# Loads of x and stores of the result in two parts of two token tiles, stores in the order of their making, last sums in two parts

## The chip, the cores and the metric

One core of a Trainium2 chip. The time is that of one execution on the device, in microseconds; the median of the runs is the kernel's time. All inputs lie in HBM when the clock starts and the result has to lie there when it stops.

## What is computed

Four layers of gated cross-attention and feed-forward over two sequences of 512 tokens, each token a row of 128 numbers in fp32. Each stage norms x, computes a branch and adds it with a gain:

```python
x = x + jnp.tanh(g_xattn[0]) * _L0_xattn_ref(_layernorm(x, axis=-1), ctx_1024, ctx_1024, mask_Bx1xSxS2_if1, ...)
x = x + jnp.tanh(g_ffn[0]) * _L0_ffn_ref(_layernorm(x, axis=-1), L0_ffn_w1, L0_ffn_b1, L0_ffn_w2, L0_ffn_b2)
...
x = x + jnp.tanh(g_xattn[3]) * _L3_xattn_ref(_layernorm(x, axis=-1), ctx_1024, L3_xattn_Wq, ...)
x = x + jnp.tanh(g_ffn[3]) * _L3_ffn_ref(_layernorm(x, axis=-1), L3_ffn_rhs)
return x
```

The layers are dense attention with a mask and an MLP (0), multi-query attention and a top-2 mixture of experts with a shared one (1), attention and a top-1 mixture (2), and three rounds of slot attention with a GRU and then a product of int8-quantised rows (3). This last one ends the program:

```python
q_lhs = jnp.clip(jnp.round(lhs / lhs_scale), -INT8_MAX, INT8_MAX).astype(jnp.int8)
q_rhs = jnp.clip(jnp.round(rhs / rhs_scale), -INT8_MAX, INT8_MAX).astype(jnp.int8)
acc = jax.lax.dot_general(q_lhs, q_rhs, (((2,), (0,)), ((), ())), preferred_element_type=jnp.int32)
return acc.astype(jnp.float32) * lhs_scale * rhs_scale
```

## The kernel before

The two sequences ("halves" in the code, index b) are 512 tokens each, held on chip as x[128 partitions, b, 4 token tiles, 128]. Partition p of tile t holds token 128 t + p. A token row is one piece of 512 bytes in HBM, so a load or store of one sequence is 256 KB in 512 such rows.

The work is cut into steps (all_steps, from line 150): a name, a sequence, an engine, an assumed duration and the steps it follows. A planner (schedule, line 308) puts every engine's steps into one fixed order, ORDERS, from the assumed durations, a table of due times for steps that need a load (LOADED, line 88) and a table of delays, LATER. The two sequences interleave on all engines. Where PE would idle, the planner puts in filler matmuls (keep_warm) that have no reader. Inside one engine the order is the program's; between engines there are only semaphores. The eight PSUM banks are dealt out by the same planner: `banks.full(name)` is a wait for PE to have filled a bank, `banks.emptied(name)` one for its reader to have drained it.

SP issues all DMAs, from one queue, in the order that is written in its block (line 726 on). Loads come first: x of sequence 0, small constants, the query weights, the context, the mask (line 738), the constant halves (740), more weights, x of sequence 1, the bias rows (747), then the weights of the later layers. After one more load in the middle of the program (line 761) SP waits for each sequence's `x_final`, sequence 0 first, stores it, and waits for both stores.

At the start DVE takes statistics of x (norm, lines 1401 and 1404, two token tiles at a time), POOL turns a variance into a reciprocal root (lines 789 and 790), behind fourteen memsets of its own (817 to 830), DVE norms the tiles (1410), converts the mask (1462, 1463), prepares the keys (1447 to 1455) and then takes sixteen maxima of scores (1537). ACT copies PSUM banks out (1232, 1236) and makes gains from the bias rows (1254).

At the end, for each sequence, DVE makes integers (integers, 1420 to 1424), PE transposes them (937) and ACT copies them out; DVE clamps them (turn, 1728), PE multiplies them (846), and quantised (1730) does the rest on DVE: four scalings of one token tile each out of PSUM (1735), and one sum of all four tiles into x (1739). The planner's order has sequence 1 before sequence 0 there. The sum waits for the drain of the bank that the last scaling signals:

```python
                last.then_inc(drained["dve"], 1)
                dve.wait_ge(*banks.emptied("out", 7, b))
                V.scalar_tensor_tensor(flat(x[:, b, :, :]), flat(xn[:, b, :, :]), gain[:, g:g + 1],
                                       flat(x[:, b, :, :]), ALU.mult, ALU.add).then_inc(x_final[b], 1)
```

Of the kernel before, what the change touches and what calls it, by code (L numbers as in the profile page):

```python
# [7 lines left out]
ALU = mybir.AluOpType  # L8
# [7 lines left out]
P = 128  # L16
B = 2
# [38 lines left out]
PACKS = {  # L56
    "attn0": [("wq", GROUPS * GR), ("wv", D), ("wo", D)],
    "ffn0": [("w1", W0), ("w2", C0 * D)],
    "attn1": [("wk", GROUPS * GR), ("wv", D), ("wq", GROUPS * GR), ("wo", D)],
    "ffn1": [("gates", E1 + 1), ("w_g", C1 * P), ("w_u", C1 * P), ("w_down", C1 * D), ("s_g", SH), ("s_u", SH),  # L60
             ("s_down", len(SHC) * D)],
    "attn2": [("wk", GROUPS * GR), ("wv", D), ("wq", GROUPS * GR), ("wo", D)],
    "ffn2": [("router", E2), ("w1", C2 * P), ("w2", C2 * D), ("bias2", D)],
    "attn3": [("wk", D), ("wv", D), ("wq", D), ("wi", 3 * D), ("wh", 3 * D), ("rhs_t", D)],
# [421 lines left out]
ORDERS, DEALT, IDLE_FILLERS = schedule()  # L486
# [41 lines left out]
def program(nc, a, out):  # L528

    with ExitStack() as ctx:  # L530
# [7 lines left out]
        x = sb("x", [P, B, T, D])  # L538
# [5 lines left out]
        cols = sb("cols", [P, cols_n])  # L544
        rows = sb("rows", [P, rows_n])
        consts = sb("consts", [P, const_n])
        ctx_t = sb("ctx_t", [P, B * CTX])
        ctx_rows = sb("ctx_rows", [CTX, B, D])
# [25 lines left out]
        ctx_4 = sb("ctx_4", [P, B, GKP])  # L574
# [81 lines left out]
        def by_tile(tile):  # L656
# [10 lines left out]


        loaded = {k: sem("loaded_" + k) for k in
                  ["x_0", "x_1", "ident", "wq0", "ctx_4", "bv", "cols", "rows", "consts", "rounded", "halves", "ctx_t", "ctx_rows", "mask"] + list(PACKS)}  # L670
        filled = sem("bank_filled")
        drained = {"act": sem("bank_drained_by_act"), "dve": sem("bank_drained_by_dve")}
        consts_made = sem("consts_made")
# [17 lines left out]
        def per_half(name):  # L691
            return [sem(f"{name}_{b}") for b in range(B)]
# [20 lines left out]
        lhs_ready = per_half("lhs_ready")  # L713
        n_ready = per_half("n_ready")
        slots_ready = per_half("slots_ready")
        x_final = per_half("x_final")
        stored = sem("stored")

# [7 lines left out]
        @block.sync  # L726
        def _(sp):
            def load_x(b):
                sp.dma_start(x[:, b, :, :], a["x"][b].rearrange("(t p) d -> p t d", p=P)).then_inc(loaded[f"x_{b}"], 16)

            wq_n = columns(PACKS["attn0"])[0]["wq"][1]
            load_x(0)
            sp.dma_start(cols[:, :], a["cols"]).then_inc(loaded["cols"], 16)
            sp.dma_start(consts[:, 0:P], a["consts"][:, 0:P]).then_inc(loaded["ident"], 16)
            sp.dma_start(packs["attn0"][:, 0:wq_n], a["attn0"][:, 0:wq_n]).then_inc(loaded["wq0"], 16)
            sp.dma_start(ctx_t[:, :], a["ctx_t"]).then_inc(loaded["ctx_t"], 16)
            sp.dma_start(consts[:, P:const_n], a["consts"][:, P:const_n]).then_inc(loaded["consts"], 16)
            sp.dma_start(mask_i[:, :, :, :], a["mask"].rearrange("b o (t p) k -> p b (o t) k", p=P))\
              .then_inc(loaded["mask"], 16)
            sp.dma_start(halves[:, :], a["halves"].bitcast(BF16)).then_inc(loaded["halves"], 16)  # L740
            sp.dma_start(packs["attn0"][:, wq_n:], a["attn0"][:, wq_n:]).then_inc(loaded["attn0"], 16)
            for i in range(B):
                sp.dma_start(ctx_4[:, i, 0:GK].rearrange("p (h k) -> p h k", h=LH),
                             a["ctx_t"][:, i * CTX:(i + 1) * CTX].unsqueeze(1).broadcast_to([P, LH, CTX]))\
                  .then_inc(loaded["ctx_4"], 16)
            load_x(1)
            sp.dma_start(rows[:, :], a["rows"].broadcast_to([P, rows_n])).then_inc(loaded["rows"], 16)
            bv_at = rows_at["bv0"][0]
            sp.dma_start(bv_cols[:, :], a["rows"][:, bv_at:bv_at + 3 * D].rearrange("o (l d) -> d (o l)", l=3),
                         allow_slow_non_contiguous=True)\  # L750
              .then_inc(loaded["bv"], 16)
            sp.dma_start(packs["attn1"][:, :], a["attn1"]).then_inc(loaded["attn1"], 16)
            sp.dma_start(packs["attn2"][:, :], a["attn2"]).then_inc(loaded["attn2"], 16)
            sp.dma_start(packs["ffn0"][:, :], a["ffn0"]).then_inc(loaded["ffn0"], 16)
            sp.dma_start(rounded_in[:, :], a["rounded"].bitcast(BF16)).then_inc(loaded["rounded"], 16)
            sp.dma_start(ctx_rows[:, :, :], a["ctx_rows"].rearrange("b k d -> k b d")).then_inc(loaded["ctx_rows"], 16)
            sp.dma_start(packs["attn3"][:, :], a["attn3"]).then_inc(loaded["attn3"], 16)
            sp.dma_start(packs["ffn1"][:, :], a["ffn1"]).then_inc(loaded["ffn1"], 16)
            for b in range(B):
                sp.wait_ge(*banks.full("out", 1, b))  # L760
            sp.dma_start(packs["ffn2"][:, :], a["ffn2"]).then_inc(loaded["ffn2"], 16)
            for b in range(B):
                sp.wait_ge(x_final[b], 1)
                sp.dma_start(out[b].rearrange("(t p) d -> p t d", p=P), x[:, b, :, :]).then_inc(stored, 16)
            sp.wait_ge(stored, 16 * B)

        def spread_keys(engine, layer, k_part, keys, ready):

# [617 lines left out]
        def _(dve):  # L1386
            V = nc.vector
# [8 lines left out]
            def norm(b, stage, h):  # L1396
                tiles = range(2 * h, 2 * h + 2)
                if stage == 0:
                    dve.wait_ge(loaded[f"x_{b}"], 16)
                for t in tiles:  # L1400
                    last = V.bn_stats(stats[:, b, t, :], x[:, b, t, :])  # L1401
                link(last)
                for t in tiles:
                    last = V.bn_aggr(mv[:, b, t, :], stats[:, b, t, :])  # L1404
                last.then_inc(var_ready[b], 1)
# [25 lines left out]
            def flat(tile):  # L1431
                return tile.rearrange("p t d -> p (t d)")
# [297 lines left out]
            def quantised(b):  # L1730
                g = GAIN_OF[7]
                dve.wait_ge(*banks.emptied("rscale"))
                dve.wait_ge(*banks.full("out", 7, b))
                for t in range(T):
                    last = V.scalar_tensor_tensor(xn[:, b, t, :], banks.bank("out", 7, b)[:, t * P:(t + 1) * P],  # L1735
                                                  route_s[:, b, 3, t:t + 1], rscale_b[:, :], ALU.mult, ALU.mult)
                last.then_inc(drained["dve"], 1)
                dve.wait_ge(*banks.emptied("out", 7, b))
                V.scalar_tensor_tensor(flat(x[:, b, :, :]), flat(xn[:, b, :, :]), gain[:, g:g + 1],  # L1739
                                       flat(x[:, b, :, :]), ALU.mult, ALU.add).then_inc(x_final[b], 1)  # L1740

            mine = {"norm": norm, "norm_end": norm_end, "integers": integers, "keys_in": keys_in, "mask_parts": mask_parts, "values_in": values_in,
                    "out_bias": out_bias, "slots_in": slots_in, "query": query, "maxima": maxima, "sum_rows": sum_rows, "spread": spread,
# [111 lines left out]
```

## Time and profile before

| | us |
|---|---|
| median of 3 runs | 345.37 |
| the three runs | 344.36, 345.45, 345.37 |
| the profiled execution | 344.06 |
| its span, first to last instruction | 342.1 |
| mean granted clock of PE, of full speed | 0.983 |

The profile is of one more execution than the three runs; its time is 344.06, of which the span is 342.1. Durations in the rows come from that execution. PE is TensorE's matmuls, DVE VectorE, ACT ScalarE, POOL GpSimd, SPq the queue of SyncE, which issues the DMAs. PE is busy 92% of the span, fillers included, DVE 65%, ACT 40%, POOL 17%. DMA works in the first 30 us, a little at 74 to 80 and at the very end.

### The profile page before, as it was taken

To read this page: it belongs to the slowest core of one execution; us is meant where nothing else is said; L and a number is where in the kernel's file an instruction comes from. 1 tells how busy PE (TensorE), PEld (TensorE's weight loads), DVE (VectorE), ACT (ScalarE), POOL (GpSimd) and SP (SyncE) were. 2 spreads that over 40 slices of the span, in tenths; PEclk is the share of its full clock that TensorE was granted. 3 is DMA by queue.
4 is the path that set the end of the run, shared out by engine and by line. 5 is a ranking of instruction groups with operands and counts; after the bars stand their busy time and mean duration, and the time that the engine had idled before them with its cause. 6 is when DMAs were issued, how large, how long until landed. Compare 5 with 4: busy or idle time off the path is not lost. (4 is left out here: it accounts for less than half of the span.)

```text
span 342.1 us, 5510 instructions
## 1 busy us (share of the span) xinstructions
PE 314.4 (92%) x2028; PEld 191.0 (56%) x2045; DVE 223.5 (65%) x634; ACT 135.5 (40%) x283; POOL 57.8 (17%) x107
## 2 busy tenths in 40 slices
PE   8889799997799999999999779999999989998983
PEld 3543544773434554656887443447769776766441
DVE  4971952769804598763588970446361889999994
ACT  1245173223366646422002255632232466757200
POOL 7131050352001021000030300012021211111220
PEclk9999999999899999999999978999999999999999
DMA  7970000021000000000000000000000000000002
GB/s 186 318 284 0 2 2 0 1 82 54 2 0 2 0 2 0 1 2 0 0 2 0 1 2 0 3 2 0 2 0 2 0 1 2 0 0 2 0 1 61
DMA packets 6958, 8.70 MB, mean 25 GB/s; under 512 B 3067, under 2 KB 5781, under 8 KB 6677
## 3 DMA queue, kind: packets, MB, share of 16 engines
q1 hardware_dynamic: 6933, 8.37, 7.3%
q8 instruction: 16, 0.26, 0.3%
q14 instruction: 9, 0.07, 0.1%
HBM read 7.84 MB, written 0.52 MB: 24 GB/s over the span
## 5 line engine op out<-in xcount | busy, mean ns | idle before, releaser
L1232 ACT ACTIVATE wide<-psum 128x512 f32<-128x512 f32 x72 | 37.2, 603 | 22.3 <-PE psum L846 22.3
L846 PE MATMUL psum<-xn_t,w_ffn 128*128 128x512 f32 (+1 forms) x88 | 41.2, 596 | 0.0
L1537 DVE TENSOR_REDUCE mx<-psum 128x4 f32<-128x308 f32 x96 | 38.2, 469 | 1.8 <-PE psum L846 1.4
L789 POOL TENSOR_SCALAR nw<-mv 128x2 f32<-128x2 f32 x32 | 7.0, 218 | 189.9 <-DVE mv L1404 189.9
L1232 ACT ACTIVATE q<-psum 128x512 f32<-128x512 f32 (+1 forms) x36 | 20.9, 595 | 27.3 <-PE psum L846 21.6
L846 PE MATMUL psum<-wide 78*128 78x386 f32 (+1 forms) x69 | 25.4, 505 | 3.2 <-DVE wide L1688 1.9
L846 PEld LDWEIGHTS psum<-early,wide 128*128 128x128 f32 x192 | 24.8, 191 | 4.9 <-issue 3.8
L846 PE MATMUL psum<-halves 128*128 128x512 bf16 x110 | 27.2, 379 | 0.4 <-issue 0.2
L1543 DVE RECIPROCAL rinv<-psum 128x64 f32<-128x64 f32 x6 | 3.3, 556 | 36.6 <-PE psum L1023 36.6
L846 PE MATMUL psum<-xn_t,early 128*128 128x512 f32 x52 | 26.5, 601 | 0.1
L846 PE MATMUL psum<-early,wide 128*128 128x128 f32 x192 | 25.3, 275 | 0.2
L846 PEld LDWEIGHTS psum<-w_ffn,wide 128*128 128x128 f32 (+1 forms) x176 | 22.4, 192 | 4.4 <-issue 3.0
L1410 DVE TENSOR_SCALAR xn<-x,mv,nw 128x128 f32<-128x128 f32 x64 | 19.0, 341 | 8.8 <-POOL nw L790 8.7
L846 PE MATMUL psum<-w_ffn,wide 128*128 128x128 f32 (+1 forms) x176 | 23.1, 276 | 0.7 <-DVE wide L1618 0.5
L790 POOL TENSOR_TENSOR nw<-nw,minus_half 128x2 f32<-128x2 f32 x32 | 23.0, 720 | 2.7
L846 PEld LDWEIGHTS psum<-xn_t,w_ffn 128*128 128x128 f32 (+1 forms) x88 | 15.3, 188 | 13.4 <-issue 10.8
L846 PEld LDWEIGHTS psum<-w_attn,q 128*128 128x128 f32 x176 | 20.8, 192 | 2.7 <-ACT wide L1232 1.7
L846 PE MATMUL psum<-w_attn,q 128*128 128x128 f32 x176 | 22.2, 277 | 0.1
L1232 ACT ACTIVATE xn_t<-psum 128x512 f32<-128x512 f32 x18 | 10.5, 596 | 26.9 <-PE psum L937 18.4
L846 PE MATMUL psum<-wide,heads_of 128*32 128x512 f32 x144 | 20.0, 630 | 0.0
L1612 DVE TENSOR_TENSOR wide<-q,psum 128x512 f32<-128x512 f32 (+1 forms) x22 | 14.7, 682 | 7.9 <-ACT q L1232 4.9
L846 PE MATMUL psum<-wide,v_cols 128*32 128x512 f32 x144 | 19.0, 600 | 0.3 <-ACT wide L1232 0.3
(222 smaller groups left out, 517.2 us busy)
## 6 DMA issues: line engine op xcount, KB each, us to landing
w_ffn<-in_ffn SPq DMA_DIRECT2D x1, 2088.5 KB, 13.6
early<-in_ffn SPq DMA_DIRECT2D x1, 1104.0 KB, 5.0
w_attn<-in_attn SPq DMA_DIRECT2D x1, 640.0 KB, 8.2
w_attn<-in_attn SPq DMA_DIRECT2D x2, 288.0 KB, 6.9
x<-in_x SPq DMA_DIRECT2D x2, 256.0 KB, 3.8
early<-in_ffn SPq DMA_DIRECT2D x1, 512.0 KB, 8.0
out<-x SPq DMA_DIRECT2D x2, 256.0 KB, 2.6
rows<-in_rows SPq DMA_DIRECT2D x1, 468.0 KB, 6.3
```

Of the source, the lines that this page charges most:

```text
L789: link(G.tensor_scalar(nw[:, b, 0, tiles], mv[:, b, tiles, 1], LN_EPS, None, ALU.add))
L790: G.tensor_tensor(nw[:, b, 2, tiles], nw[:, b, 0, tiles], minus_half[:, tiles], ALU.pow)\
L846: return nc.tensor.matmul(out_, lhs, rhs, start=start, stop=stop, **kw)
L1232: A.activation(dst, banks.bank(*name)[0:rows_, 0:cols_], fn, **kw).then_inc(drained["act"], 1)
L1410: last = V.tensor_scalar(xn[:, b, t, :], x[:, b, t, :], mv[:, b, t, 0:1], nw[:, b, 2, t:t + 1], ALU.subtract, ALU.mult)
L1537: last = V.tensor_reduce(mx[:, b, t, lane_heads(g)], banks.bank("max", layer, b, t, g)[:, 0:GK].rearrange("p (h k) -> p h k", k=CTX), AX.X ...
L1543: V.reciprocal(rinv[:, b, :, :], banks.bank("sum_t", layer, b).rearrange("p (t h d) -> p t h d", t=T, h=H)[:, :, :, 0])\
L1612: V.tensor_tensor(wide[0:r, b, at_, :], act_s[k % 2][0:r, b, :], banks.bank("up", b, k)[0:r, :], ALU.mult)\
```

## The change

A load of x for one sequence becomes two loads of two token tiles, each with a semaphore; the statistics of two tiles wait for their own load. The stores become two per sequence, each of two tiles, in the order in which DVE's own list has the sequences. In quantised the second scaling signals `scaled_back`; the last sum is split into two of two tiles, the first waiting for that signal, the second for the drain as before, and each signals x_final.

```diff
             def load_x(b):
-                sp.dma_start(x[:, b, :, :], a["x"][b].rearrange("(t p) d -> p t d", p=P)).then_inc(loaded[f"x_{b}"], 16)
+                for h in range(2):
+                    tiles = slice(2 * h, 2 * h + 2)
+                    sp.dma_start(x[:, b, tiles, :], a["x"][b].rearrange("(t p) d -> p t d", p=P)[:, tiles, :])\
+                      .then_inc(loaded[f"x_{b}_{h}"], 16)
...
-            for b in range(B):
-                sp.wait_ge(x_final[b], 1)
-                sp.dma_start(out[b].rearrange("(t p) d -> p t d", p=P), x[:, b, :, :]).then_inc(stored, 16)
-            sp.wait_ge(stored, 16 * B)
+            for b in (b for phase, b, _ in ORDERS["dve"] if phase == "quantised"):
+                for h in range(2):
+                    tiles = slice(2 * h, 2 * h + 2)
+                    sp.wait_ge(x_final[b], h + 1)
+                    sp.dma_start(out[b].rearrange("(t p) d -> p t d", p=P)[:, tiles, :], x[:, b, tiles, :]).then_inc(stored, 16)
+            sp.wait_ge(stored, 2 * 16 * B)
...
                 if stage == 0:
-                    dve.wait_ge(loaded[f"x_{b}"], 16)
+                    dve.wait_ge(loaded[f"x_{b}_{h}"], 16)
...
                     last = V.scalar_tensor_tensor(xn[:, b, t, :], banks.bank("out", 7, b)[:, t * P:(t + 1) * P],
                                                   route_s[:, b, 3, t:t + 1], rscale_b[:, :], ALU.mult, ALU.mult)
+                    if t == 1:
+                        last.then_inc(scaled_back[b], 1)
                 last.then_inc(drained["dve"], 1)
-                dve.wait_ge(*banks.emptied("out", 7, b))
-                V.scalar_tensor_tensor(flat(x[:, b, :, :]), flat(xn[:, b, :, :]), gain[:, g:g + 1],
-                                       flat(x[:, b, :, :]), ALU.mult, ALU.add).then_inc(x_final[b], 1)
+                for h in range(2):
+                    tiles = slice(2 * h, 2 * h + 2)
+                    if h:
+                        dve.wait_ge(*banks.emptied("out", 7, b))
+                    else:
+                        dve.wait_ge(scaled_back[b], 1)
+                    V.scalar_tensor_tensor(flat(x[:, b, tiles, :]), flat(xn[:, b, tiles, :]), gain[:, g:g + 1],
+                                           flat(x[:, b, tiles, :]), ALU.mult, ALU.add).then_inc(x_final[b], 1)
```

The instructions of PE, ACT and POOL are the same, in the same order. Line numbers behind the edit are six or more higher in the changed kernel (1735 is 1741, 1739 is 1752, 764 is 770).

SP's queue at the start of the program, before:

```order
L729 DMA x<-in_x 128x4x128
L733 DMA cols<-in_cols 128x32
L734 DMA consts<-in_consts 128x128
L735 DMA early<-in_attn 128x160
L736 DMA ctx_t<-in_ctx_t 128x154
L737 DMA consts<-in_consts 128x112
L738 DMA early<-in_mask 128x8x77
```

and in the changed kernel:

```order
L732 DMA x<-in_x 128x2x128 x2
L737 DMA cols<-in_cols 128x32
L738 DMA consts<-in_consts 128x128
L739 DMA early<-in_attn 128x160
L740 DMA ctx_t<-in_ctx_t 128x154
L741 DMA consts<-in_consts 128x112
L742 DMA early<-in_mask 128x8x77
```

Everything behind the load of x, the mask among it, stands one issue later; the same happens once more at x of sequence 1.

SP's queue at the end, before:

```order
L758 DMA w_ffn<-in_ffn 128x4177
L761 DMA early<-in_ffn 128x2208 [waits bank_filled]
L764 DMA out<-x 128x4x128 [waits x_final_0]
L764 DMA out<-x 128x4x128 [waits x_final_1]
L530 UNCONDITIONAL_BRANCH [waits stored]
```

and in the changed kernel:

```order
L762 DMA w_ffn<-in_ffn 128x4177
L765 DMA early<-in_ffn 128x2208 [waits bank_filled]
L770 DMA out<-x 128x2x128 [waits x_final_1] x2
L770 DMA out<-x 128x2x128 [waits x_final_0] x2
L530 UNCONDITIONAL_BRANCH [waits stored]
```

The stores are four, and sequence 1's come before SP's wait for sequence 0.

DVE at the end of the program, before; the first scalings and sum are sequence 1's, nothot_t is the clamp of sequence 0:

```order
L1735 SCALAR_TENSOR_TENSOR xn<-psum,route_s,rscale_b 128x128 [waits bank_filled,bank_drained_by_act]
L1735 SCALAR_TENSOR_TENSOR xn<-psum,route_s,rscale_b 128x128 x3
L1739 SCALAR_TENSOR_TENSOR x<-xn,gain,x 128x512 [waits bank_drained_by_dve]
L1728 TENSOR_SCALAR nothot_t<-nothot_t 128x512 [waits bank_drained_by_act]
L1735 SCALAR_TENSOR_TENSOR xn<-psum,route_s,rscale_b 128x128 [waits bank_filled,bank_drained_by_act]
L1735 SCALAR_TENSOR_TENSOR xn<-psum,route_s,rscale_b 128x128 x3
L1739 SCALAR_TENSOR_TENSOR x<-xn,gain,x 128x512 [waits bank_drained_by_dve]
```

and in the changed kernel:

```order
L1741 SCALAR_TENSOR_TENSOR xn<-psum,route_s,rscale_b 128x128 [waits bank_filled,bank_drained_by_act]
L1741 SCALAR_TENSOR_TENSOR xn<-psum,route_s,rscale_b 128x128 x3
L1752 SCALAR_TENSOR_TENSOR x<-xn,gain,x 128x256 [waits scaled_back_1]
L1752 SCALAR_TENSOR_TENSOR x<-xn,gain,x 128x256 [waits bank_drained_by_dve]
L1734 TENSOR_SCALAR nothot_t<-nothot_t 128x512 [waits bank_drained_by_act]
L1741 SCALAR_TENSOR_TENSOR xn<-psum,route_s,rscale_b 128x128 [waits bank_filled,bank_drained_by_act]
L1741 SCALAR_TENSOR_TENSOR xn<-psum,route_s,rscale_b 128x128 x3
L1752 SCALAR_TENSOR_TENSOR x<-xn,gain,x 128x256 [waits scaled_back_0]
L1752 SCALAR_TENSOR_TENSOR x<-xn,gain,x 128x256 [waits bank_drained_by_dve]
```

The first half's sum still stands behind all four scalings; only its wait is for an earlier one.

## Rows read from the trace of the kernel before

**Rows 1.** Chain that ended last, 335 to 342: start us, us, what
```profile
335.68 0.21 DVE nothot_t L1728
...
336.03 0.40 PE psum L846 x4
...
336.52 1.14 DVE xn L1735 x4
...
337.68 0.75 DVE x L1739
```

**Rows 2.** Waits of SP: who waited for whom, us in total, times, longest
```profile
SPq L764 <- DVE x L1739: 264.3, 1, 264.3
...
SPq L530 <- DMA out<-x: 2.3, 1, 2.3
```

**Rows 3.** Timeline, 333 to 342: start us, us, instruction, [idle before <-releaser]
```profile
333.77 1.12 DVE L1735 SCALAR_TENSOR_TENSOR xn<-psum,route_s,rscale_b 128x128 f32<-128x128 f32 x4
...
338.46 0.95 SPq L764 DMA_DIRECT2D out<-x  x2
```

**Rows 4.** Windows 339.0 to 341.7: busy us, PEclk, DMA share, GB/s
```profile
339.00:339.40 0.40, 0.00 (x0) 0.00 (x0) 0.00 (x0) 0.00 (x0) 0.00 (x0) 1.00 0.00 1
339.40:341.30 1.90, 0.00 (x0) 0.00 (x0) 0.00 (x0) 0.00 (x0) 0.00 (x0) 0.91 0.93 275
341.30:341.70 0.40, 0.00 (x0) 0.00 (x0) 0.00 (x0) 0.00 (x0) 0.00 (x0) 0.50 0.01 3
```

**Rows 5.** Timeline, 0 to 14, columns as in rows 3
```profile
3.64 0.43 SPq L738 DMA_DIRECT2D early<-in_mask  x1
...
3.92 0.95 POOL L830 MEMSET nothot_t<- 128x1024 bf16 x1
...
4.06 0.25 DVE L1404 BATCH_NORM_AGGREGATE mv<-stats 128x2 f32<-128x6 f32 x2
...
4.92 0.22 POOL L789 TENSOR_SCALAR nw<-mv 128x2 f32<-128x2 f32 x1
...
5.97 0.60 DVE L1410 TENSOR_SCALAR xn<-x,mv,nw 128x128 f32<-128x128 f32 x2 [1.01 <-POOL nw L790]
...
7.49 0.31 DVE L1462 TENSOR_SCALAR mask_b<-early 128x308 bf16<-128x308 int32 x1
...
8.41 0.17 DVE L1447 TENSOR_REDUCE lane_mask<-consts 128x4 f32<-128x16 f32 x1
...
8.87 0.24 DVE L1450 CAST k_hi<-k_t 128x154 fp32r<-128x154 f32 x1 [0.29 <-ACT k_t L1236]
```

**Rows 6.** Line 764, the stores: duration ns min/median/max, and landing
```profile
L764 SPq DMA_DIRECT2D out<-x x2: 398/452/507, 338.5 to 338.9; - x2
...
DMA to landing us min/median/max: 2.4/2.6/2.8
```

**Rows 7.** Lines 1735 and 1739: duration ns min/median/max, first and last start
```profile
L1735 DVE SCALAR_TENSOR_TENSOR xn<-psum,route_s,rscale_b x8: 340/343/350, 333.8 to 337.3; 128x128 f32<-128x128 f32 x8
...
L1739 DVE SCALAR_TENSOR_TENSOR x<-xn,gain,x x2: 752/752/752, 334.9 to 337.7; 128x512 f32<-128x512 f32 x2
```

**Rows 8.** DMA issues, from the page: KB, us from issue to landing
```profile
early<-in_mask SPq DMA_DIRECT2D x1, 308.0 KB, 3.7
...
cols<-in_cols SPq DMA_DIRECT2D x1, 16.0 KB, 2.5
```

**Rows 9.** Windows: length, busy us of PE, PEld, DVE, ACT, POOL, PEclk, DMA, GB/s
```profile
12.00:20.00 8.00, 6.17 (x50) 4.19 (x47) 7.96 (x26) 0.93 (x3) 0.00 (x0) 1.00 1.02 383
...
88.00:91.75 3.75, 1.89 (x28) 1.02 (x24) 3.12 (x9) 2.06 (x4) 0.00 (x0) 1.00 0.00 0
...
201.00:207.70 6.70, 5.88 (x36) 2.88 (x40) 2.89 (x8) 3.23 (x7) 0.00 (x0) 0.50 0.00 0
```

**Rows 10.** Timeline, 12 to 22, columns as in rows 3
```profile
13.12 0.21 ACT L1254 ACTIVATE gain<-rows 128x8 f32<-128x8 f32 x1 [1.00 <-DMA rows<-in_rows]
...
20.17 1.02 PE L846 MATMUL psum<-mask_t,halves 77*128 77x512 bf16 x4 [0.38 <-ACT mx_t L1232]
```

More of the change, by code:

```diff
@@ L669, in program @@
         loaded = {k: sem("loaded_" + k) for k in
-                  ["x_0", "x_1", "ident", "wq0", "ctx_4", "bv", "cols", "rows", "consts", "rounded", "halves", "ctx_t", "ctx_rows", "mask"] + list(PACKS)}
+                  ["x_0_0", "x_0_1", "x_1_0", "x_1_1", "ident", "wq0", "ctx_4", "bv", "cols", "rows", "consts", "rounded", "halves", "ctx_t", "ctx_rows", "mask"] + list(PACKS)}
         filled = sem("bank_filled")
@@ L715, in program @@
         slots_ready = per_half("slots_ready")
+        scaled_back = per_half("scaled_back")
         x_final = per_half("x_final")
```

## Prediction

> **What bounds the kernel now.** The change touches both ends of the program and nothing between, so I read the two ends. The chain that ended last [rows 1] shows the tail: PE multiplies sequence 0's quantised rows at 336.03, DVE scales the four token tiles from 336.52, and one 512-wide sum on DVE runs 337.68 to 338.43. SP's waits [rows 2] and the timeline [rows 3] show what hangs on that. SP waited 264.3 us for L1739 and then issued both stores together at 338.46. Sequence 1 was finished first (its four scalings start at 333.77, its sum is done at 335.68), but SP stands on sequence 0's semaphore, so a finished 256 KB waits 2.8 us for nothing. After 338.46 + 0.95 = 339.41 SP waits 2.3 us, to 341.71, for the landings. The span ends 0.4 later.
>
> The windows of the last microseconds [rows 4] cut that end into three: 0.94 us from the first issue to the first bytes (nothing moves before 339.40), 1.90 us at a 0.93 share of the 16 DMA engines and 275 GB/s, which is the whole 0.524 MB, and 0.41 us from the last bytes (341.30) to SP's release. So 1.90 of the 3.3 us behind DVE is bandwidth over both sequences' bytes.
>
> At the front I read the timeline [rows 5]. DVE has its first x statistics done at 4.06 + 0.25 = 4.31, but POOL is in its last memset until 3.92 + 0.95 = 4.87 and takes the statistics at 4.92. POOL releases DVE at 5.97, not the load of x.
>
> **The change, part by part.**
>
> Stores in finishing order. Sequence 1's parts leave at about 335.3 and 335.8, and are through before 338, beside DVE and PE work. What remains behind the end of DVE is 256 KB in place of 512: half of 1.90, a gain of 0.95 us. Each issue takes 0.40 to 0.51 us [rows 6] and SP has nothing else to do then; the two more issues cost nothing there.
>
> Last sums in two parts. A 128x128 scaling takes 343 ns, the 128x512 sum 752 [rows 7]; the slope is 409/384 = 1.07 ns a column, so a 256-wide sum takes about 480. Four scalings take 1.13 [rows 1, 3]: independent ones start (1.13 - 0.343)/3 = 0.26 apart, that is 0.08 before the last ends, while the sum, which waits for the last scaling, starts 0.03 after it. The first half now waits for the second scaling only, so it starts at 337.65 - 0.08 = 337.57 and ends at 338.05; the second starts 0.40 later and ends at 338.45. Against 338.43 the split costs 0.02: the fixed cost of one more instruction (752 - 2 x 480, that is 0.21) is paid by the two overlaps, 0.11 and 0.08. The same holds at sequence 1, where DVE's own clamp of sequence 0 (L1728, on the chain at 335.68 [rows 1]) is next. Bounds: -0.05 each, and +0.2 each if neither overlap comes. I take 0 to 0.05 for both together.
>
> Store in two parts. The first part is issued at 338.05 + 0.03 = 338.08, in place of 338.46: 0.38 earlier. The second follows an issue later, at 338.53 (the two issues before stood 0.44 apart), with its sum done at 338.45. First bytes at 338.08 + 0.94 = 339.02, then 256 KB without a gap, 0.95, to 339.97; release at 340.38. Against 341.71: 1.33 us, of which 0.95 are bytes and 0.38 the earlier first part. With the splits' cost I take **1.3** for the tail. Bounds: 1.35 above; below, the landing of the second part. The trace has no 128 KB store; its 256 KB stores landed 2.4 and 2.8 us after issue [rows 6], the second because it queued behind the first. With 2.8 from 338.53 the gain is 0.4, with 2.4 it is 0.8. I take 1.85: 0.94 + 0.48 + 0.41 = 1.83, and the undisturbed 2.4 less half its bytes' time, 0.48, gives 1.9.
>
> The Trainium skill, "DMA: Bandwidth & Descriptors", section "Anatomy of one DMA — SWDGE (gpsimd) path", gives a fixed cost of about 2.0 us and then bytes over 436 GB/s, and lays most of the 2 us on the write's receipt; an estimate by it puts a 128 KB store at 2.3 us and the tail's gain at 0.9 instead of 1.3. The trace differs in the split: 0.41 us passed between the last bytes and the release [rows 4].
>
> Loads of x in two parts. The first half would be there about 0.5 us sooner (half of 256 KB), but POOL takes it at 4.92 either way: gain 0. The extra issue pushes every later load by about 0.48 us, those behind x_1 by 0.95. One of them has no slack. The mask is issued at 3.64 and lands 3.7 later, at 7.34 [rows 8], and DVE converts it at 7.49 without a pause [rows 5]. It now lands at about 7.82, DVE starts at 7.86, 0.37 late. Behind the four conversions stand the 8.41 reduction and then 0.29 us of idle before 8.87, where ACT's k_t is awaited: that absorbs 0.27 of it, and the cast starts **0.1** late. Who waits for that: DVE is busy 7.96 of 8.00 us in 12 to 20 [rows 9], so its sixteen maxima end 0.1 later, then ACT's mx_t, then PE at 20.17 [rows 10]. I carry all of it to the end. Bounds: 0, and 0.7 (the mask slipping by both extra issues' time, 0.95, less the 0.27). The others are covered: the bias rows land 0.95 later, and ACT, which waits for them at 13.12 [rows 10], has nothing behind that but mx_t, made after the maxima; x_1's statistics stand behind the sixteen maxima too.
>
> Sum: 1.3 - 0.1 = **1.2 us**. The profiled execution took 344.06 (span 342.1 and 2.0 around it); it would take 342.9. It lies 1.3 below the median, 345.37, near the lowest run, 344.36. From the median: **344.2 us**, 0.35% less. The bound between faster and the same is 0.3%, 1.04 us here, about what a measurement of this kernel can tell from no change.
>
> **The rivals.**
>
> *A store has a price that halving does not cut.* If a 128 KB store lands in 2.4 us, like the 256 KB one (and a 16 KB load took 2.5 [rows 8]), the second part is there at 340.93: tail 0.8, net 0.7, 344.7, the same. Against it: the 1.90 us of saturated engines, which must shrink with the bytes. For it: small loads are no quicker, though they queued behind others. The Trainium skill's page named above, "DMA: Bandwidth & Descriptors", stands on this side.
>
> *The late mask costs more.* Loads share the engines, and the mask's row comes from a queue with no second x part in it. At the bound of 0.7 the net is 0.6: 344.8, the same. For it: DVE's backlog from 8.87 on has no other slack. Against: the bytes ahead of the mask are the same.
>
> *Slower: PE's clock falls once more.* The granted clock is 1.00 in 12 to 20, where PE was busy 6.17 of 8 us waiting for DVE's maxima. It fell after 88 to 91.75, where PE was busy 1.89 of 3.75, and once more at 201, where it stayed at 0.50 for 6.7 us [rows 9], which is the 1.2 GHz level. If DVE's delay stretches PE's waits at 12 to 20, or moves a later stretch over the edge, work at half speed costs half the low stretch: 3.35 us for one like 201's. Net +2.15: 347.5, slower. It decides from a low stretch of 4.5 us (2.24 lost: the gain and 1.04). Against: PE is far busier there than before the falls, and the delay is 0.1 us. The other sign is as possible: a low stretch shortened gives 1 to 2 us more than forecast, near 342.9.
>
> *The early half of x counts.* Only if POOL were not what releases DVE; the memset's end excludes it but for hundredths. Up to 0.5 more: 343.7, faster.
>
> That the stores don't change order is excluded: SP's own order shows sequence 1 first.
>
> **How the numbers follow.** Forecast 0.52 (343.9 to 344.3, 344.2 the likeliest). Flat store price 0.20, late mask 0.13, both same. Slower clock 0.06; shorter low stretch 0.05; early x 0.04. Faster 0.52 + 0.05 + 0.04 = 0.61, less 0.03 for a forecast that lands just inside the bound: 0.58. Same 0.20 + 0.13 + 0.03 = 0.36. Slower 0.06. The range: above to a tail of 0.4 with the mask at 0.4, 345.4; below, 343.1, to the best tail (1.35, nothing at the front) and a median near the low runs, since the four executions shown spread over 1.4 us. Outside lie the clock cases and a little more.
>
> **What would show it.** Right: SP's wait for x_final ends near 335.3; four issues, two of them near 338.1 and 338.5; DMA busy about 0.95 us at the end, SP released some 1.9 us after its last issue; DVE's two 256-wide sums ending within 0.05 of where the one did; POOL still taking x's statistics at 4.92; a DVE idle of about 0.3 before the mask conversion, and the cast 0.1 late. Wrong: a last store that lands 2.4 us or more after its issue, PE or DVE further behind than 0.1 by 20 us, or a low-clock stretch that the kernel before did not have.

## The result and the profile after

| | before | changed |
|---|---|---|
| median, us | 344.33 (22 runs) | 342.85 (22 runs) |
| lowest and highest | 342.68, 345.45 | 341.51, 345.40 |
| profiled execution, us | 344.06 | 342.90 |
| its span | 342.1 | 341.0 |

The ratio is 0.9956, with a 95% interval of 0.9939 to 0.9973: less time, by 0.44% or 1.5 us, and clear of no change. It is not clear of the 0.3% that the prediction takes as its bound for faster: the interval begins at 0.27%. The three runs of before that stood ahead of the prediction had a median of 345.37; nineteen more brought it to 344.33.

The tail of the changed kernel, from its timeline (columns as in rows 3), the waits of SP, the four stores by line, and the windows of the last transfer (columns as in rows 4), in this order:

```profile
334.46 0.69 ACT L1238 ACTIVATE nothot_t<-psum,round_col 128x512 bf16<-128x512 f32 x1 [2.74 <-PE psum L943]
335.00 0.87 DVE L1752 SCALAR_TENSOR_TENSOR x<-xn,gain,x 128x256 f32<-128x256 f32 x2
335.50 3.64 SPq L770 DMA_DIRECT2D out<-x  x4
335.79 0.28 DVE L1734 TENSOR_SCALAR nothot_t<-nothot_t 128x512 bf16<-128x512 bf16 x1
...
336.71 1.13 DVE L1741 SCALAR_TENSOR_TENSOR xn<-psum,route_s,rscale_b 128x128 f32<-128x128 f32 x4 [0.64 <-PE psum L852]
337.75 0.87 DVE L1752 SCALAR_TENSOR_TENSOR x<-xn,gain,x 128x256 f32<-128x256 f32 x2
```

```profile
SPq L770 <- DVE x L1752: 264.0, 2, 261.8
...
SPq L530 <- DMA out<-x: 1.4, 1, 1.4
```

```profile
L770 SPq DMA_DIRECT2D out<-x x4: 372/434/471, 335.5 to 338.7; - x4
...
DMA to landing us min/median/max: 1.9/1.9/1.9
```

```profile
336.40:337.60 1.20, 0.20 (x4) 0.03 (x1) 0.89 (x4) 0.00 (x0) 0.00 (x0) 1.00 0.77 219
339.10:340.20 1.10, 0.00 (x0) 0.00 (x0) 0.00 (x0) 0.00 (x0) 0.00 (x0) 1.00 0.84 238
340.20:340.60 0.40, 0.00 (x0) 0.00 (x0) 0.00 (x0) 0.00 (x0) 0.00 (x0) 1.00 0.01 1
```

Against [rows 1 to 4]: sequence 1's stores leave from 335.50 and move between 336.4 and 337.6, beside DVE's and PE's work. DVE's last sum ends at 337.75 + 0.87 = 338.62; 0.5 us later bytes move, 1.1 us long in place of 1.9, and the span ends at 340.98. Before, DVE ended at 338.43 and the span at 342.10. From DVE's last end to the span's end there were 3.67 us; now 2.36. That is 1.31 us. The split of the last sums is free: first scaling to last sum took 1.91 us before (336.52 to 338.43) and takes 1.91 now (336.71 to 338.62).

The span is only 1.1 shorter, because DVE's end moved back by 0.19. That isn't from the front, since by 20 us PE stands where it stood. It appears behind the low stretch of PE's clock at 201: from 20 us up to there PE's matmuls stand in both profiles within 0.04 us of each other, but for the 0.3 us inside the low stretch at 92. The front, from the timeline:

```profile
2.82 0.49 DVE L1407 BATCH_NORM_STATS2 stats<-x 128x6 f32<-128x128 f32 x2 [1.71 <-DMA x<-in_x]
...
4.93 0.22 POOL L795 TENSOR_SCALAR nw<-mv 128x2 f32<-128x2 f32 x1
...
7.51 0.31 DVE L1468 TENSOR_SCALAR mask_b<-early 128x308 bf16<-128x308 int32 x1
...
9.04 0.24 DVE L1456 CAST k_hi<-k_t 128x154 fp32r<-128x154 f32 x1 [0.45 <-ACT k_t L1242]
```

The statistics start at 2.82 in place of 3.54, and POOL takes them at 4.93, as before [rows 5]. The mask was issued at 4.13, landed in 3.3 us and not in 3.7, and did not delay DVE at all in this execution. The cast is 0.17 late because ACT's k_t is, and k_t because PE's key matmul is. That in turn is PE's clock, whose level the matmuls' own durations show (the trace has no clock record before the first rise, and prints 1.00 there): the warm-up matmuls, line 852, 4 to 8 us:

```profile
L852 PE MATMUL psum<-wide x12: 379/634/634, 3.7 to 7.9; 128*128 128x512 bf16 x12
```

They take 634 ns at the low level, 1.2 GHz, and 379 at 2.4 GHz. The change from one to the other came at 6.4 us in the profile before and at 6.8 here, and PE's instructions are the same up to there. By 20.18 PE starts its first scores as it did at 20.17 [rows 10]. The 0.17 is not absorbed by a wait: from the cast to the first scores pass 11.00 to 11.14 us in this profile and the twelve of the experiments, and 11.30 in that of before, which happened to lose there what the changed kernel had lost already.

### The profile page after: what moved, and what is told of

The parts are those of the page before. It is cut to its first block and busy times, and to the rows that moved or that the text cites. A ratio compares the mean times of both kernels' runs of the same rounds, so it can differ in the third digit from the quotient of the medians.

```text
span 341.0 us, 5516 instructions
## 1 busy us (share of the span) xinstructions
PE 314.7 (92%) x2028; PEld 190.9 (56%) x2045; DVE 223.8 (66%) x636; ACT 135.6 (40%) x283; POOL 57.9 (17%) x107
## 3 DMA queue, kind: packets, MB, share of 16 engines
HBM read 7.84 MB, written 0.52 MB: 25 GB/s over the span
## 5 line engine op out<-in xcount | busy, mean ns | idle before, releaser
L852 PE MATMUL psum<-wide,heads_of 128*32 128x512 f32 x144 | 20.4, 640 | 0.0
```

The lines of the kernel that those rows point to most:

```text
L852: return nc.tensor.matmul(out_, lhs, rhs, start=start, stop=stop, **kw)
```

## The experiments

All of them are told by the same few readings. "Mask" is the start of the mask's conversion on DVE, "scores" that of PE's first score matmul (mask_t,halves), "DVE end" the end of the last sum, "tail" the span's end less DVE's end, "low clock" the time at half clock before DVE's end, from windows of granted clock. The ratio is against the kernel before on the same chip, whose median was 344.45 for e1 to e4, 344.20 for e5 to e7, 343.79 for e8 to e11 and 344.17 for e12; medians of different groups are therefore not to be subtracted. The columns from mask to tail are from one profiled execution each.

| kernel | median | ratio, 95% | mask | scores | low clock | DVE end | tail |
|---|---|---|---|---|---|---|---|
| before | 344.33 | | 7.49 | 20.17 | 10.2 | 338.43 | 3.67 |
| changed | 342.85 | 0.9956, 0.9939 to 0.9973 | 7.51 | 20.18 | 10.2 | 338.62 | 2.36 |
| e1 order of stores | 343.18 | 0.9965, 0.9946 to 0.9985 | 7.48 | 19.61 | 17.1 | 339.47 | 2.72 |
| e2 change, x whole | 343.07 | 0.9952, 0.9930 to 0.9973 | 7.64 | 20.28 | 10.2 | 338.79 | 2.37 |
| e3 x in parts only | 343.90 | 0.9986, 0.9972 to 1.0000 | 7.94 | 20.07 | 6.8 | 337.73 | 3.66 |
| e4 parts, old order | 344.40 | 0.9998, 0.9977 to 1.0020 | 8.25 | 20.39 | 17.1 | 340.37 | 3.47 |
| e5 POOL freed | 343.17 | 0.9972, 0.9952 to 0.9992 | 7.90 | 20.03 | 10.2 | 339.56 | 2.48 |
| e6 change again | 343.36 | 0.9970, 0.9950 to 0.9991 | 8.74 | 20.87 | 10.2 | 339.33 | 2.36 |
| e7 change, spare | 339.67 | 0.9862, 0.9839 to 0.9886 | 8.08 | 20.39 | 0 | 335.70 | 2.36 |
| e8 before, spare | 340.79 | 0.9907, 0.9886 to 0.9928 | 7.49 | 20.19 | 0 | 335.46 | 3.65 |
| e9 order, spare | 339.99 | 0.9885, 0.9863 to 0.9907 | 7.49 | 19.61 | 0 | 334.91 | 2.73 |
| e10 x in parts, spare | 340.94 | 0.9917, 0.9893 to 0.9941 | 7.49 | 19.98 | 0 | 335.27 | 3.66 |
| e11 change, spare | 339.42 | 0.9875, 0.9851 to 0.9898 | 7.84 | 19.98 | 0 | 335.29 | 2.36 |
| e12 best | 339.12 | 0.9852, 0.9819 to 0.9885 | 7.49 | 19.62 | 0 | 334.86 | 2.37 |

**e1, the order of the stores alone.**

```diff
-            for b in range(B):
+            for b in (b for phase, b, _ in ORDERS["dve"] if phase == "quantised"):
                 sp.wait_ge(x_final[b], 1)
```

> Only the order of the two whole stores is changed (sequence 1's before sequence 0's); loads, sums and store sizes are those of the kernel before. Theory (the time behind DVE's last sum is bytes plus fixed parts): sequence 1's 256 KB leave at about 335.7 and are gone by 338; behind DVE's end remain 0.03 + 0.94 + 0.95 + 0.41 = 2.3 us in place of 3.28, so 0.95 to 1.0 us less, 0.28% of the time. Rival (a store has a price that does not shrink with what is queued): the last store lands 2.8 us after its issue as before, and the gain is only the one issue, 0.44 us. Rival (the gain came from the earlier loads or from something in the middle): no gain here, ratio 1.000.

The tail fell from 3.67 to 2.72, by 0.95: the theory's number, and the price rival's 0.44 is out. Each whole store now lands by itself in 2.3 us; before it was 2.4 and 2.8 [rows 6]:

```profile
L764 SPq DMA_DIRECT2D out<-x x2: 394/396/399, 336.7 to 339.5; - x2
...
DMA to landing us min/median/max: 2.3/2.3/2.3
```

Its DVE end, though, was 1.0 later than before's, with no edit there. What differs is the table's low clock column.

**e2, the change with x loaded whole** (the load part taken back, the rest kept).

```diff
-                for h in range(2):
-                    tiles = slice(2 * h, 2 * h + 2)
-                    sp.dma_start(x[:, b, tiles, :], a["x"][b].rearrange("(t p) d -> p t d", p=P)[:, tiles, :])\
-                      .then_inc(loaded[f"x_{b}_{h}"], 16)
+                sp.dma_start(x[:, b, :, :], a["x"][b].rearrange("(t p) d -> p t d", p=P)).then_inc(loaded[f"x_{b}"], 16)
...
-                    dve.wait_ge(loaded[f"x_{b}_{h}"], 16)
+                    dve.wait_ge(loaded[f"x_{b}"], 16)
```

> The change without its load part: x is loaded whole per sequence; the stores and last sums are those of the change. Theory (the split loads are worth nothing, since POOL takes the first statistics at 4.92 either way, and whatever they cost is absorbed before 25 us): as fast as the change, 1.3 us less than before behind DVE's end (1.98 us from DVE's last end to the release in place of 3.28), ratio to before 0.996. Rival (the split loads bring the 0.2 us by which the median fell more than the 1.3 of the tail): 0.2 to 0.4 us slower than the change. Rival of the forecast (the later mask costs 0.1): 0.1 us faster than the change, with the key cast at 8.87 and not 9.04.

Tail 2.37, ratio 0.9952: the stores and sums carry the whole gain, as far as twelve runs with an interval of 0.2% to each side can tell. The cast stood at 9.15 with whole loads, behind a k_t that was done at 9.04, so the change's 9.04 was not the loads' doing.

**e3, the loads alone** (the first hunk of the change and its wait, nothing else).

> The load part alone: x in two parts, all at the end as before. Theory: no difference, ratio 1.000 within 0.1%; the first statistics on DVE start near 2.8 instead of 3.54, POOL still takes them at 4.92, and by 25 us every engine stands where it stood. The tail is 3.28 us from DVE's last end to SP's release. If the early microseconds differ from before, it is by the moment at which PE's clock rises (the warm-up matmuls go from 427 to 216 ns apart at 6.44 before, at 6.79 in the change), and the key cast moves with that moment and not with the mask's landing, which should be near 7.4. Rival (the late mask): the cast is 0.1 or more late whenever the clock rises. Rival (the earlier x counts): 0.2 to 0.5 us faster.

Tail 3.66, as before. The ratio's interval ends at 1.0000, which settles neither a small gain nor none; e10 asks again. Here DVE did wait for the mask:

```profile
7.94 0.32 DVE L1465 TENSOR_SCALAR mask_b<-early 128x308 bf16<-128x308 int32 x1 [0.37 <-DMA early<-in_mask]
```

**e4, parts in the old order** (e2 with `for b in range(B)` around the stores).

> Last sums and stores in two parts as in the change, but SP waits for sequence 0 first, as before; x is loaded whole. All 512 KB then leave behind DVE's first half sum of sequence 0. Theory: the first bytes move 0.38 us sooner than before, and the rest is 1.90 us of transfer as before, if four issues at 0.44 us keep ahead of it (the fourth is issued 1.32 us after the first, its bytes due 1.43 after the first's): 2.9 us from DVE's last end to the release, 0.35 us less than before, ratio 0.999. Rival (each further store costs its own time on the engines): as slow as before or 0.1 to 0.3 us slower.

Tail 3.47, 0.20 less and not 0.35. SP's four issues in the timeline and the stores' windows (columns as in rows 4) show why:

```profile
339.50 0.87 DVE L1749 SCALAR_TENSOR_TENSOR x<-xn,gain,x 128x256 f32<-128x256 f32 x2
340.00 1.99 SPq L767 DMA_DIRECT2D out<-x  x4
```

```profile
341.40:341.80 0.40, 0.00 (x0) 0.00 (x0) 0.00 (x0) 0.00 (x0) 0.00 (x0) 1.00 0.87 255
341.80:342.20 0.40, 0.00 (x0) 0.00 (x0) 0.00 (x0) 0.00 (x0) 0.00 (x0) 1.00 0.86 241
342.20:342.60 0.40, 0.00 (x0) 0.00 (x0) 0.00 (x0) 0.00 (x0) 0.00 (x0) 1.00 0.83 224
```

Four issues take 1.99 us, 0.50 each where I had 0.44, and 128 KB take 0.48 to move at the rate of [rows 4]: the engines were busy 0.83 to 0.87 where the two whole stores kept them at 0.93. The queue's issue rate and the bytes are about even at 128 KB, so parts in the old order give little. That smaller parts would give less is an estimate from these numbers; none were run.

**e5, POOL freed at the front.**

```diff
-            G.memset(comb_t[:, :, :].bitcast(F32), 0.0)
-            G.memset(nothot_t[:, :, :], 0.0).then_inc(zeros_made, 1)
...
-            for phase, b, args in ORDERS["pool"]:
+            for i, (phase, b, args) in enumerate(ORDERS["pool"]):
+                if i == 2:
+                    G.memset(comb_t[:, :, :].bitcast(F32), 0.0)
+                    G.memset(nothot_t[:, :, :], 0.0).then_inc(zeros_made, 1)
                 mine[phase](b, *args)
```

> The change, with POOL's last two memsets (comb_t and nothot_t, 0.95 us each) moved behind the first norm of sequence 0, so that POOL can take the first statistics at about 3.6 and not 4.92. Theory (the front is held by POOL first, and by the mask's landing, ACT's table load and PE's key matmul right behind it): DVE norms x's first tiles near 4.7 instead of 5.97, so the early half of x now shows; but ACT's k_t, the mask conversion and the key cast stand where they stood (k_t at 8.4 to 8.6, the cast near 9), and the maxima start at 12.1 to 12.3 as before. Time as the change, within 0.2%. Rival (the x chain is what the front waits for): the maxima start 0.5 us or more sooner and the time falls by 0.5 us, 0.15%.

```profile
3.88 0.22 POOL L795 TENSOR_SCALAR nw<-mv 128x2 f32<-128x2 f32 x1 [0.78 <-DVE mv L1411]
...
4.93 0.60 DVE L1417 TENSOR_SCALAR xn<-x,mv,nw 128x128 f32<-128x128 f32 x2 [0.53 <-POOL nw L796]
...
5.85 0.95 POOL L839 MEMSET comb_t<- 128x1024 f32 x1
...
5.93 1.91 DVE L1417 TENSOR_SCALAR xn<-x,mv,nw 128x128 f32<-128x128 f32 x2 [0.40 <-POOL nw L796]
...
6.74 0.95 POOL L840 MEMSET nothot_t<- 128x1024 bf16 x1
...
7.54 0.39 ACT L1243 ACTIVATE k_t<-psum,cols 128x154 f32<-128x154 f32 x1
...
7.90 0.32 DVE L1469 TENSOR_SCALAR mask_b<-early 128x308 bf16<-128x308 int32 x1
...
9.03 0.24 DVE L1457 CAST k_hi<-k_t 128x154 fp32r<-128x154 f32 x1
```

DVE norms x a whole microsecond earlier, at 4.93 in place of 5.98, and the cast stands where it stood. The early x shows once POOL is out of its way, and is then lost at the mask, which landed at 7.87. It isn't lost at k_t, as I had expected: k_t was done at 7.54 + 0.39 = 7.93, a microsecond before the cast, because PE's clock rose at 3.9 here. Nor is the test clean. The norms of the other two tiles took 1.84 and 1.65 us where they take 0.34 in every other profile, and ended at 7.84, beside the two memsets that were moved to 5.85 to 7.69. Even an earlier mask would have found DVE busy until then. That the memsets hold the norms up is read from this one profile and not tested. Scores at 20.03, ratio 0.9972, no faster than the change.

**e6, the change again.**

> The changed kernel once more, with nothing altered, for two questions: what its gain is on this chip beside the kernel before, and what moves the time from one execution to the next. Theory: from DVE's last end to the span's end 2.36 us again, as in the other executions with these stores, whatever the time is; ratio to before 0.995 to 0.997. The place of DVE's last end varies between executions by 1 to 2 us with PE's low-clock stretches (10.2 us of them in the change's first profile, 17.1 in two others), whose place follows the moment at which the clock first rose. Rival (the spread is noise of the start and end of an execution): DVE's last end is at 338.6 again within 0.2 whatever the clock does.

The tail is 2.36 again, the theory's number. DVE's end is 0.71 later than in the first profile with the same 10.2 us of low clock, so the theory's account of the spread was incomplete: this time it was the mask.

```profile
8.74 0.32 DVE L1468 TENSOR_SCALAR mask_b<-early 128x308 bf16<-128x308 int32 x1 [1.16 <-DMA early<-in_mask]
...
9.87 0.24 DVE L1456 CAST k_hi<-k_t 128x154 fp32r<-128x154 f32 x1
```

```profile
20.87 0.81 PE L852 MATMUL psum<-mask_t,halves 77*128 77x512 bf16 x3 [0.21 <-ACT mx_t L1238]
```

It landed at 8.7, and the scores started at 20.87, 0.69 late, which the end shows whole.

**e7, spare matmuls in PE's waits.** The change and 17 fillers:

```diff
+            SPARE = {(0, 1, 2): 1, (1, 1, 2): 1, (1, 1, 3): 5, (0, 2, 0): 3, (0, 2, 2): 2, (0, 2, 3): 5}
+
             def maxima(b, layer, t):

-                bks = [start_unit("max", layer, b, t, g) for g in range(LANES)]
+                bks = [start_unit("max", layer, b, t, 0)]
+                for _ in range(SPARE.get((b, layer, t), 0)):
+                    mm(bks[0], halves[:, 0:P], halves[:, 0:S])
+                bks += [start_unit("max", layer, b, t, g) for g in range(1, LANES)]
```

> The change, with 17 more filler matmuls of 512 columns (results unused) inside PE's waits at the maxima of layers 1 and 2: into the first bank of a group as soon as it is free, while PE waits for the other three. PE idles there 0.5 to 1.3 us at a time, and both low-clock stretches before the end began there. Theory (the low clock follows those idle waits, and costs what separates executions: 337.7 us at DVE's last end with 6.8 us of low clock, 338.4 to 338.8 with 10.2, 339.5 and 340.4 with 17.1): one or both low stretches go or shrink, DVE ends near 336.5 to 337.5, and the time falls 1 to 2 us below the change. Rival (PE isn't on the path in the low stretches, or the fillers delay the score matmuls behind them): no difference or 0.3 to 1 us slower, the low stretches unchanged.

More than the 1 to 2 us below the change that I expected: 339.67 against 343.36 for e6 on the same chip, and against 344.20 for the kernel before. The five runs lie within 0.65 us where before's 23 spread over 2.9; e11, the same kernel again, will show a wider spread. The windows of the changed kernel, then those of e7 (columns as in rows 9):

```profile
88.00:92.00 4.00, 2.14 (x29) 1.27 (x29) 3.39 (x9) 2.06 (x4) 0.00 (x0) 1.00 0.00 0
...
92.10:95.50 3.40, 3.40 (x28) 1.47 (x20) 1.15 (x3) 2.15 (x5) 0.00 (x0) 0.50 0.02 5
201.30:208.20 6.90, 6.35 (x40) 3.25 (x44) 2.64 (x7) 2.96 (x6) 0.00 (x0) 0.51 0.00 0
```

```profile
88.00:92.00 4.00, 3.69 (x34) 1.74 (x35) 3.39 (x9) 2.06 (x4) 0.00 (x0) 1.00 0.02 4
199.00:203.00 4.00, 3.65 (x31) 1.66 (x31) 3.36 (x9) 2.00 (x5) 0.00 (x0) 1.00 0.00 0
```

PE is busy 3.69 of 4 us where it was busy 2.14, and the clock stays at its upper level, 2.4 GHz, to DVE's end in this execution.

**e8 to e11, the parts of the change on this steadier ground.** e8 is the kernel before with the 17 fillers, e9 is e1 with them, e10 is e3 with them, e11 is e7 again.

> The kernel before with the 17 spare filler matmuls, and nothing of the change: the base on which the parts of the change can be told apart, because without low-clock stretches five runs of the change with them lay within 0.65 us. Theory: no low clock, 339.67 + 1.3 of tail - 0.2 to 0.3 of loads = 340.7 to 341.0, spread under 1 us, 3.67 us from DVE's last end to the span's end. Rival (the spare matmuls work only together with the change): low stretches again and 343 or more.

> The spare matmuls and the order of the two whole stores alone. Theory: 0.95 us less than the kernel before with spare matmuls (0.28%): 339.8 to 340.0. Rival: 0.44 us less.

> The spare matmuls and the split loads of x alone. The mask's conversion on DVE began at 7.48, 7.49, 7.64 and 8.25 in the profiles with whole loads, at 7.51, 7.90, 7.94, 8.08 and 8.74 with split ones: 0.3 later on the mean, and the change's second profile carried 0.7 us of it to PE's first scores (20.87 against 20.17). Theory now: the split loads cost 0.2 to 0.4 us against the kernel before with spare matmuls, since nothing hides the mask. Rival (what I took from the first profile, all absorbed before 25 us): no difference within 0.1 us. Rival (the 0.9986 of the loads alone was a gain): 0.3 to 0.5 us faster.

> The change with the spare matmuls again, beside its parts on one chip. Theory: 1.3 us of tail less what the loads cost, 1.0 to 1.2 us faster than the kernel before with spare matmuls, 339.5 to 339.9; the two measured parts and the halves of stores and sums (0.35) add up to it. Rival (0.44% from the 22 runs is the change's own gain): 1.5 us or more.

By medians on one chip: order -0.80, loads +0.15, the whole change -1.37. By profiles: tail -0.92, +0.01 and -1.29. And between scores and DVE's end the four profiles and e7's have 315.27, 315.30, 315.29, 315.31 and 315.31 us, whatever part of the change is in: the middle of the program is untouched to 0.04 us. The medians still carry the start of the scores, which moves between 19.6 and 20.4; six runs don't average that out, so that the loads' +0.15 is a possible cost, not a shown one (e3 alone had 0.9986, the other way). The whole change came out 0.2 above my expectation's upper end for the gain, within the same scatter.

Where the spare matmuls gain is seen by laying DVE's instructions of e8 beside the same ones of before. From 37 to 93 us they stand within 0.03 us of each other, from 102 to 195 e8's are 0.91 to 0.94 earlier, and from 214 to the end 2.96 to 3.00. The gain arises at the two low stretches and nowhere else, 0.9 us for the first (3.4 us long) and 2.0 for the second (6.8 us). The kernel before says the same without any spare matmuls: of its 78 runs beside e1 to e12, the 17 with a mean granted clock of 0.986 to 0.989 have a median of 343.16 us, the 7 at 0.974 one of 345.47.

The spare matmuls don't hold the clock up in every execution. Of the 34 runs of e7 to e12, 31 had a mean granted clock of 0.995 or more; one of e9, one of e10 and one of e11 had 0.990, 0.989 and 0.991 and took 340.78, 341.88 and 341.00 us, 0.8 to 1.6 above their kernels' medians. With that one e11 spread over 1.8 us, where the same kernel had spread over 0.65 in e7.

**e12, the version that the runs point to.** e7 with x loaded whole, and the mask ahead of cols, ident and consts in SP's queue:

```diff
             load_x(0)
-            sp.dma_start(cols[:, :], a["cols"]).then_inc(loaded["cols"], 16)
-            sp.dma_start(consts[:, 0:P], a["consts"][:, 0:P]).then_inc(loaded["ident"], 16)
...
-            sp.dma_start(consts[:, P:const_n], a["consts"][:, P:const_n]).then_inc(loaded["consts"], 16)
...
             sp.dma_start(mask_i[:, :, :, :], a["mask"].rearrange("b o (t p) k -> p b (o t) k", p=P)).then_inc(loaded["mask"], 16)
+            sp.dma_start(cols[:, :], a["cols"]).then_inc(loaded["cols"], 16)
+            sp.dma_start(consts[:, 0:P], a["consts"][:, 0:P]).then_inc(loaded["ident"], 16)
+            sp.dma_start(consts[:, P:const_n], a["consts"][:, P:const_n]).then_inc(loaded["consts"], 16)
```

> What the runs point to: the spare matmuls, the stores in order and in two parts with the last sums in two parts, x loaded whole, and SP's queue at the start reordered so that the mask stands fourth (behind x, the query weights and the context) and not seventh. Theory: the mask conversion on DVE at 7.5 in every execution, PE's first scores at 19.6 to 20.2 by the moment the clock rises, 315.3 us from there to DVE's last end as in the five profiles with spare matmuls, 2.36 us of tail: a span of 337.3 to 337.9, and 339.1 to 339.4 as the median, 0.1 to 0.3 below the change with spare matmuls. Rival (something that now lands later, the identity or the column constants, holds PE's first transpose at 7.9 or ACT's k_t): the scores start later than 20.3 and it is no faster than the change with spare matmuls.

```profile
332.95 1.13 DVE L1743 SCALAR_TENSOR_TENSOR xn<-psum,route_s,rscale_b 128x128 f32<-128x128 f32 x4 [0.64 <-PE psum L849]
333.99 0.87 DVE L1754 SCALAR_TENSOR_TENSOR x<-xn,gain,x 128x256 f32<-128x256 f32 x2
334.49 0.89 SPq L767 DMA_DIRECT2D out<-x  x2
```

The mask's conversion at 7.49, scores at 19.62, 315.24 us to DVE's end, tail 2.37; median 339.12, five runs within 0.37 us, ratio to before 0.9852 (0.9819 to 0.9885). It is faster than the kernel before and the changed one. Its lead over e11, 0.3, is across two chips and mostly the early scores of one profile; that moving the mask is worth it in the mean is not shown.

## Why the prediction was right and wrong

*Stores in finishing order: right.* 0.95 forecast; 0.95 in e1's tail, 0.92 in e9's.

*Last sums in two parts, free: right.* 476 ns each where I had 480, and 1.91 us from first scaling to last sum on both sides.

*Stores in two parts, 0.38: right.* 2.72 to 2.37 is 0.35, and a 128 KB store landed in 1.9 where the sum had 1.85. The rival of a flat price (2.4 from issue, tail gain 0.8) is out by the row of the four landings. With it goes the reading by the Trainium skill's page "DMA: Bandwidth & Descriptors", by whose fixed 2.0 us and bytes the estimate was 2.3; that page's formula is for DMAs issued from POOL, these are SP's. The tail as a whole: 1.3 forecast, 1.31 measured. It is 2.36 or 2.37 in six of the seven profiles with these three parts; e5's has 2.48, and there the last store's issue took 0.60 us instead of 0.47.

*Loads of x, early half worth nothing: right*, and for the reason given. e5 took that reason away and found the mask's landing behind it.

*The mask 0.37 late, the cast 0.1 late, all carried: the chain was right, the size isn't shown.* In the eight profiles in which the mask's conversion and not k_t came last before the cast, the cast started 1.12 to 1.14 us after the first conversion, and the scores 11.0 after the cast, so that a delay of the cast is carried. The first conversion started at 7.48 to 8.25 with whole loads (six profiles, mean 7.64; 7.48 or 7.49 in four) and at 7.49 to 8.74 with split ones (seven, mean 7.93): 0.29 later, and PE's first scores at 20.04 and 20.21 on the mean, 0.17 later. But one execution differs from the next by more, since the mask took 3.3 to 4.6 us to land; and what the cast waits for is mask or k_t, whichever is later, k_t moving with the moment of PE's first clock rise. The profile of before happened to show the mask exactly in time, from which I worked out an exact delay that no single execution has. My rival of a late mask at up to 0.7 was real: e6 is such an execution. But so is e4, with whole loads, whose mask was converted at 8.25: a late mask isn't the split's doing alone.

*The clock rival: the price and the place were wrong.* I took a low stretch of 6.7 us to cost half its length, 3.35 us, and named 12 to 20 us as where it might appear. It never did. The stretches sit at the same two places, near 90 and 200 us, in every kernel without spare matmuls (they begin at 89.6 to 92.6 and at 198.8 to 205.3), 6.8 to 17.1 us of them in sum. Against 315.3 us without any, scores to DVE's end took 317.7 with 6.8, 318.3 to 319.5 with 10.2, and 319.9 to 320.0 with 17.1: 0.3 to 0.4 us for each us of low clock, and by e8 beside before 0.3. My half would hold if PE were all that the path waits for; that it isn't is the likely reason for the difference, not a tested one.

*The level: this is the step that failed.* The forecast gain, 1.2 us, lies inside the measured interval (0.93 to 2.1 us), and the profiled execution, 344.06, came down to 342.90, where the working had put it, at 342.9. That the two agree so well is partly luck: the 0.1 that I charged for the mask did not occur in this execution, and DVE's end moved back by 0.19 at a low stretch of the clock, which the working does not have. What I then did was to take the gain from the median of three, 345.37: "From the median: 344.2 us". Two of those three are among the slowest of the 22 runs, whose median is 344.33. From there the same gain gives 343.1; measured was 342.85, 0.25 under the low end of my range, 343.1, and 1.35 under the forecast. I had noted that the profiled execution lay 1.3 below the median and that four executions spread over 1.4 us, and charged that to the range's low end only in part. The four executions together have a mean of 344.8, and that, with a range of 1.4 around it before any doubt on the change is added, was the level to start from. That three runs gave a median 1.0 above that of 22 was bad luck; that they could was readable from the four. What executions differ by is now known in large part, low clock and the mask, but for those three runs no clock is on record. The remaining 0.3 of the miss is the gain itself, 1.5 against 1.2, a difference that the interval of 0.93 to 2.1 doesn't show to be real.

*What stays open.* The ratio of 22 runs says 1.5 us, 0.3 more than the tail less the mask's delay; e6 says 1.0, e11 against e8 1.4. The first two lie within each other's intervals, and I take 1.1 to 1.4 for the change's own worth. Why one store's issue in e5 took 0.13 us longer was not tried.

## What to carry to other kernels

Read the end of a kernel as a chain of its own: from the last compute instruction to the end of the span, split into issue, first byte, bytes and release. What can be moved ahead of that instruction is worth its bytes, here 0.95 us for one line that puts the queue's waits in the order in which results are made, and it can be read from one profile (0.95 in e1, 0.92 in e9) although the runs spread over 3 us.

When executions of a kernel spread more than the change is worth, find what differs between two profiles before experimenting on the change. Filling PE's short waits in two stages gave 0.9% (e8 against before) to 1.1% (e7 against e6), where the change gave 0.30% (e6) to 0.44%, and made 31 of 34 runs agree with the others of their kernel within 0.9 us.

## What was not expected of the hardware

PE's clock first rose at 6.4 and 6.8 us in the profiles before and after, at 3.9 in e5's and at 7.2 in e7's, with the same instructions of PE up to there; e11's, the same kernel as e7's, had 5.2. The Trainium skill, "TensorE: Matmul & The Clock Gate", Part 1, says that this moment varies between runs of one kernel; the runs here agree. PE fell to 1.2 GHz at 92.1 us in the changed kernel although its longest wait in the 4 us before was 1.3 us: it was busy 2.14 of those 4 us.

A load of 308 KB in 1024 short rows, issued into a queue with the same neighbours, landed in 3.3 to 4.6 us in the thirteen profiles that have it at that place, where the 128 KB stores at the quiet end took 1.8 to 2.0 every time.
